# Two weighted slots at each of two points of the tile loop instead of one at each of four

## The reference, cut to what matters

```python
q = (feat @ Wq).reshape(N, H, D)          # N 3125, H 4, D 64
k = (feat_c @ Wk).reshape(N, H, D)
v = (feat_c @ Wv).reshape(N, H, D)
e = jnp.einsum('ehd,ehd->eh', k[src], q[dst]) / jnp.sqrt(jnp.float32(H * D))
ex = jnp.exp(e - emax[dst])               # emax: maximum over the edges of one dst
m = v[src] * (ex / denom[dst])[..., None] # denom: sum of ex over the edges of one dst
ft2 = jax.ops.segment_sum(m, dst, num_segments=N).reshape(N, F)
```

## Time and profile before

| | before |
|---|---|
| median of three executions | 2643.17 us |
| lowest and highest of them | 2631.5 and 2644.66 us |
| profiled execution, device time | 2620.13 us |
| span of its profile | 2618.4 us |
| busy: PE, DVE, ACT, POOL | 79%, 67%, 57%, 46% |
| granted TensorE clock, mean | 0.851 |
| tile loop | from about 118 to 1757 us of the span |

### The profile page before, as it was taken

The page is one execution under the profiler, slowest core; times in us unless marked ns, Lnnn a source line. Parts: engine busy times, 40 slices in busy tenths (PEclk is TensorE's granted clock), DMA queues, the critical chain, the costliest instruction groups (busy, mean ns, idle before and its releaser), DMA issues. The chain is left out here.

```text
span 2618.4 us, 45726 instructions
## 1 busy us (share of the span) xinstructions
PE 2074.0 (79%) x12641; PEld 1454.6 (56%) x12641; DVE 1757.7 (67%) x3515; ACT 1479.9 (57%) x4918; POOL 1215.0 (46%) x1183
## 2 busy tenths in 40 slices
PE   7747777777786667778777777857989986999998
PEld 3423333333332255556555555545778876999997
DVE  7457777777777676676667566677979985444443
ACT  2246555665665636566566555666865534555554
POOL 0456555555566445555555555524820001444443
PEclk9868788888888758787888877867989987999999
DMA  7666666666666556666666556647920118222221
GB/s 215 201 181 201 189 187 183 197 186 194 186 195 198 173 161 178 175 191 177 195 177 192 176 169 196 188 125 228 313 95 25 31 42 288 38 35 35 33 36 20
DMA packets 227731, 406.06 MB, mean 155 GB/s; under 512 B 58972, under 2 KB 129809, under 8 KB 227521
## 3 DMA queue, kind: packets, MB, share of 16 engines
q0 software_dynamic: 83712, 250.84, 34.5%
q1 hardware_dynamic: 120852, 116.88, 14.9%
q10 hardware_dynamic: 22957, 35.95, 3.7%
HBM read 345.66 MB, written 58.83 MB: 154 GB/s over the span
## 5 line engine op out<-in xcount | busy, mean ns | idle before, releaser
L826 POOL DMA_INDIRECT ring<-kv_tab,idx x904 | 918.4, 1016 | 709.0 <-issue 361.3
L1170 ACT ACTIVATE val<-ring,val 128x64 f32<-128x64 f32 x1808 | 477.2, 342 | 8.2 <-DVE part L928 7.3
L885 DVE TENSOR_TENSOR ring<-ring,tile_bank 128x1024 f32<-128x1024 f32 x226 | 274.4, 1214 | 64.5 <-ACT tile_bank L1160 41.6
L890 DVE TENSOR_REDUCE score<-ring 128x16 f32<-128x1024 f32 x226 | 268.3, 1212 | 0.0
L922 DVE TENSOR_TENSOR val<-val 128x1040 f32<-128x1040 f32 x113 | 140.3, 1242 | 184.0 <-ACT val L1170 174.5
L1286 PE MATMUL tile_bank<-q_win,spread 128*128 128x256 f32 x452 | 176.2, 476 | 108.3 <-DVE val L914 50.6
L2240 POOL DMA_INDIRECT out<-e_yw,to_row x56 | 120.7, 2155 | 222.3 <-DVE e_yw L2267 206.1
L2316 PE MATMUL e_h<-e_xT,e_now 128*128 128x128 f32 x1792 | 211.9, 277 | 0.7 <-DVE e_now L2257 0.7
L2316 PEld LDWEIGHTS e_h<-e_xT,e_now 128*128 128x128 f32 x1792 | 207.2, 194 | 1.1 <-DVE e_now L2257 1.1
L2331 PE MATMUL e_yps<-e_now,e_hT 128*128 128x256 f32 x896 | 202.5, 379 | 0.0
L2225 POOL DMA_INDIRECT xr<-rows,from_row x56 | 57.5, 1027 | 289.8 <-issue 289.5
(11 more groups left out here) (424 smaller groups left out, 5004.7 us busy)
## 6 DMA issues: line engine op xcount, KB each, us to landing
g_ring<-parts SPq DMA_DIRECT2D x137, 260.0 KB, 4.4
parts<-part ACTq DMA_DIRECT2D x113, 260.0 KB
q_win<-q_tab SPq DMA_DIRECT2D x226, 128.0 KB
e_w_all<-L_ffn_W SPq DMA_DIRECT2D x16, 1024.0 KB, 11.7
ring<-kv_tab,idx POOLq DMA_INDIRECT x904
kv_tab<-kv_t SPq DMA_DIRECT2D x25, 224.0 KB
blocks<-t SPq DMA_DIRECT2D x216, 5.0 KB
blocks<-t SPq DMA_DIRECT2D x216, 0.0 KB
```

The lines of the kernel that those rows point to most:

```text
L826: pool.indirect_dma_start(out=ring[:, n % RING, g * L + e, :], out_offset=None, in_=t.kv_tab, in_offset=bass.IndirectOffsetOnAxis(ap=idx[n ...
L885: dve.tensor_tensor(k, k, bcast(q_ps[g].unsqueeze(1), 128, L, F), ALU.mult).then_inc(q_read[g], 1)
L890: dve.tensor_reduce(score[:, :, g, :], ring[:, n % RING, g * L:(g + 1) * L, 0:F].rearrange("p s (h d) -> p s h d", h=HG), AX.X, ALU.add).t ...
L1170: one = act.activation(val[n % 2][:, 1, e, h, 0:DG], ring[:, n % RING, L + e, F + h * DG:F + (h + 1) * DG], ACT.Copy, scale=val[n % 2][:, ...
```

## The change

ScalarE weighs slots 0 and 1 of tile `n` at the end of the quarter c = 3 of tile `n`, and slots 2 and 3 at the end of c = 0 of the next tile. Nothing is weighed at the end of c = 1 and c = 2. Instructions, buffers and semaphores are the same; `act_val_ready` is still raised by the last instruction of slot 3.

```diff
@@ -1256,8 +1256,10 @@
                         settle_nodes(n + AHEAD)
                     if c == 3 and n < TILES:
                         weigh_slot(n, 0)
-                    elif c < 3 and 0 < n <= TILES:
-                        weigh_slot(n - 1, 1 + c)
+                        weigh_slot(n, 1)
+                    elif c == 0 and 0 < n <= TILES:
+                        weigh_slot(n - 1, 2)
+                        weigh_slot(n - 1, 3)
             for j in range(2):
                 act.wait_ge(part_out[j], 16 * len(range(j, TILES, 2)))
```

## The result

The changed kernel takes 2748.15 us (median; 2739.64 to 2751.89), the kernel before on the same chip 2639.59 us (2631.5 to 2644.66): a ratio of 1.0446, 95% interval 1.0405 to 1.0486. The forecast was 2584 us, with a range from 2532 to 2665. The sign was wrong, and the time lies 83 us above the range. The medians differ by 109 us, the two profiled executions by 126: the span is 2744.4 us. The tile loop, from the first L885 to the end of the last L922, runs from about 120 to 1884 us and takes 1764 us in place of 1640, so 124 of the 126 us are in it.

A forecast was written before the change was run, and what follows sets the result against it. The prediction took a chain through TensorE, ScalarE's phi and slot 3, and VectorE to bound the tile loop. Terms -89 - 33 + 38 + 25 = -59 us from 2643 gave 2584 us, range 2532 to 2665.

The forecast's parts named there:

- The loop: Tile loop: the chain TensorE, phi, slot 3, exponentials, VectorE, TensorE sets the period, 14.44 us against 14.5 a tile.
- the 7.71 us: From L1286's start to ScalarE's phi of c = 2: some two us of work, the rest unexplained, carried over.
- GpSimd's wait: GpSimd's wait for slot 3 before gathering, 340.1 us in 77 times: the longest wait, claimed not to matter.
- Slot 3 and L922, -89 us: VectorE no longer waits at L922 for slot 3, so L885 starts sooner: 1.25 us in 71 tiles, -89 us.
- Slot 3 ahead of L1160, -33 us: On ScalarE, slot 3 leaves the chain ahead of L1160, saving 0.95 us in 35 tiles: -33 us.
- The phis of c = 0 and c = 1, +38 and +25 us: Slots moved ahead of these ScalarE phis delay them: +38 us in 71 tiles, +25 us in 26 short ones.
- Gathers, nothing: GpSimd's gathers run eight in a row; the data are needed three tiles later either way: no effect.
- Rival 1: No change: TensorE's own pace rules, L922's wait moves to L885 and phi waits grow; 2643 us, chance 0.20.
- Rival 2: Slower: TensorE waits for the later phis of c = 0 and c = 1, net +57; 2700 us, chance 0.16.
- Rival 3: Eight gathers in a row hold TensorE back, 5 us in 40 tiles; some 2780 us, chance 0.02.
- the short tile: Tile around the phi at 728.74, ScalarE never idle for long: taken as evidence against a general hold by gathers.

The follow-up runs named there:

- late_release_2: Changed kernel with group 1's gathers held until ScalarE has written the rows of c = 2, where the kernel before takes 2666.26 us: 2659.45 us, ratio 0.9971.
- before_again: The kernel before, unaltered, run again on the chip where it takes 2666.26 us: ratio 0.9997.
- before_bunched_2: The kernel before, with GpSimd waiting for slot 3 ahead of both groups, so eight gathers run in a row: ratio 1.0335.
- late_release: Changed kernel with group 1's gathers held until the rows of c = 2 are written, on a chip where the kernel before takes 2227.94 us: ratio 1.0008.

## Why the prediction was wrong, point by point

**The loop.** "Of the 7.71 us the rows show only some two of work ... the change doesn't touch them, and I carry them over": this is the step that failed, and with it the term "nothing" for the gathers. The 7.71 us end 1.48 us after the series of gathers, and the change sets when the series begins and how long it is. The reading was loose as well: TensorE works without a break from 1389.83 to 1393.93, 4.10 us, and what stays unexplained is the 3 us over which its last three matmuls are drawn out, 2.34 of them idle. The chain added up to 14.44 us and to the mean tile, but any way round a loop adds up to its period, so the sum was no evidence for its links. The link that held the unexplained part was more than half of it.

**GpSimd's wait.** "The longest entry ... looks like the one that matters and is none." It was the link that closed the loop: slot 3 released the series. The argument, that no engine waits for the rows themselves, was sound and missed the point. The series acts on TensorE while it runs, not by the data that it brings.

**Slot 3 and L922, -89 us.** The wait went, as said. The time did not: with the release put back 0.3% came (0.0 to 0.6%, so it may be nothing), of 2.2% forecast in all. After, L885 follows L1160 by 0.31 us in the tile shown, as forecast (0.34), but waits for L1160 35 times (40 up to the loop's end), not over 60.

**Slot 3 ahead of L1160, -33 us.** In `late_release_2` slot 3 is out of the loop and `where_read` takes its place in it. A tile takes 14.96 us on average there and 14.97 us in `before_again`, so no such gain is shown.

**The phis of c = 0 and c = 1, +38 and +25 us.** `late_release_2` has them and is not slower. Their cost can be no more than what slot 3 and the shorter series give back. They are not told apart by a run.

**Gathers, nothing.** Eight in a row cost 3.35% in `before_bunched_2`, some 89 us, as much as the largest term of the sum and of the other sign. The reason given, that the tile's data are needed three tiles later, is true, and doesn't bear on what the transfers do to TensorE.

**Rival 1** named the sign that L885 would inherit L922's wait. `late_release_2` shows it in part: that wait grows from 19.2 to 79.3 us, and a pace that doesn't start with L1286 is right too. But the waits for phis, which it had growing by what L922 loses, went from 542 to 507 us. **Rival 2** falls as an account of the time. Its sign is there in part: from 150 to 1757 us TensorE's waits for phis and for L697 and L1197 grow from 109 us in `before_again` to 160 in `late_release_2`, which is no slower, and from 111 us in before to 157 after. **Rival 3** is what happened, with phis waiting up to 11.2 us until a series of eight is over. Its price was 40 tiles by 5 us, less a gain of 59; in the two tiles shown the gap between series is 1.16 us longer (5.33 for 4.17), by 113 tiles 131 us, against the 124 us of the loop. This product takes the two stretches as typical; the tiles scatter much more than that. The prediction took 1397.5, where ScalarE's phi starts, for the moment at which TensorE got going again; TensorE had run a matmul at 1396.01, before the last gather was over. Rival 3 had 0.02, for the short tile in which no phi was held. That tile lies in a series of 16 gathers, from 722.00 on, and the phi at the end of it waited 7.91 us, until 743.16, when the last gather ran: the row was read as the absence of a hold, and the hold came later in the same series.

## What to carry to other kernels

When a chain explains the period but one link has no work in it, look at what every other engine does in that stretch, and at what starts and ends there, before forecasting with it: here a series of gathers ended 0.3 to 2.3 us ahead of the phi in 47 of its 91 waits of over 2 us. Moving the last reader of a buffer also moves what the buffer's release starts; a refill that nobody waits for can still cost what it does to others while it runs. And measure on more than one chip: eight gathers in a row cost 3.35% on one and nothing that can be told (1.0017, 0.9995 to 1.0038) on another.

## What the runs showed of the hardware

The same program takes 2227 to 2230 us on four chips, and 2631, 2640 and 2666 us in the three comparisons on the other kind. The difference is in the tile loop (1253 us for `late_release` on the first kind, 1688 on the second; what lies outside it takes 980 and 976 us). On the first kind TensorE works on through over a hundred gathers in a row, and the stretch from 150 to 1350 us moves 243 GB/s. On the second its matmuls are drawn out while packets of the gathers are in flight, the phis come behind the series, and the same stretch moves 185 GB/s in before and 176 in after. A gather takes GpSimd the same on both, 1016 ns on average in before and 1014 in `late_release` on the first kind. The instruction queues carry 81 and 129 packets on either, so it is no difference in how much code is loaded. The traces differ in one more thing: for the same program, `late_release`, the first kind has 37,591 records of semaphores and the second 23,045, with all 45,726 instructions in both. This is a likely reason why so many releasers are "remote" or "issue" on the second. Whether the writing of these records takes part in the hold isn't tested. What else sets the chips apart no run here shows.
